# Message stages of a two-layer graph network: row loads and stores of sums issued one per step instead of in groups

## The reference

```python
edge_index = jnp.stack([src, dst])
h = jnp.maximum(_layernorm(x, axis=-1), 0.0)
x = x + _L0_gnn_ref(h, node_vec1, edge_attr_16, edge_attr_4, src, dst, ...)
h = jnp.maximum(_layernorm(x, axis=-1), 0.0)
x = x + _L1_gnn_ref(h, edge_attr_3, edge_attr_64, ..., edge_index)
# the core of layer 1 (layer 0 is alike, with the mean instead of a sum over 32)
w = jax.nn.relu(edge_feature @ W_fc1) @ W_fc2
xs, xv = s[dst], v[dst]
tp = jnp.concatenate([w0 * xs, w3 * einsum(xv, sh1), w1 * xs * sh1, w2 * xv, w4 * cross(xv, sh1)], axis=-1)
agg = jax.ops.segment_sum(tp, src, num_segments=N) / DENOM
```

## Time and profile before

| | |
|---|---|
| time, median of 3 runs | 10098.53 us (10094.6 to 10099.18) |
| the profiled execution, span | 12165.8 us |
| layer 0 messages, stretch read | 3000 to 7500 us |
| layer 1 messages, stretch read | 8600 to 11800 us |
| mean granted TensorE clock | 0.763 |

### The profile page before, as it was taken

The page is one execution under the profiler, slowest core; times in us unless marked ns, Lnnn a source line. Parts: engine busy times, 40 slices in busy tenths (PEclk is TensorE's granted clock), DMA queues, the critical chain, the costliest instruction groups (busy, mean ns, idle before and its releaser), DMA issues. The chain is left out here.

```text
span 12165.8 us, 170335 instructions
## 1 busy us (share of the span) xinstructions
PE 7197.2 (59%) x31160; PEld 4885.2 (40%) x31160; DVE 7321.5 (60%) x20980; ACT 4968.3 (41%) x16490; POOL 7606.9 (63%) x7069
## 2 busy tenths in 40 slices
PE   4444444444555555555555555676777777777778
PEld 3222222222222222222222222454666666766667
DVE  6444444445665666656656665665667666766664
ACT  2333333333333333333333333343555555545543
POOL 3666666656666666766666666555666666666660
PEclk7555555557777777777777777787888888888889
DMA  2222222223333333433333335444444434434365
GB/s 79 72 72 74 72 71 73 73 69 107 114 114 113 116 112 115 117 113 114 116 113 115 113 116 109 121 144 126 121 118 120 119 116 121 119 115 119 115 112 166
DMA packets 850560, 1315.71 MB, mean 108 GB/s; under 512 B 252608, under 2 KB 651712, under 8 KB 850368
## 3 DMA queue, kind: packets, MB, share of 16 engines
q0 software_dynamic: 337920, 667.48, 19.8%
q1 hardware_dynamic: 438416, 547.38, 15.3%
q10 hardware_dynamic: 74160, 100.15, 2.5%
HBM read 862.45 MB, written 914.08 MB: 146 GB/s over the span
## 5 line engine op out<-in xcount | busy, mean ns | idle before, releaser
L1425 POOL DMA_INDIRECT feat_m<-feat_tab,rows_m x3712 | 4206.2, 1133 | 2025.3 <-issue 1291.5
L1524 PE MATMUL pair<-prod_m,hot_m 128*128 128x160 f32 x14848 | 2529.9, 332 | 924.5 <-DVE prod_m L1743 644.4
L1524 PEld LDWEIGHTS pair<-prod_m,hot_m 128*128 128x128 f32 x14848 | 2359.4, 214 | 1095.3 <-issue 1095.0
L1557 ACT ACTIVATE prod_m<-part_m,rows_m 128x64 f32<-128x64 f32 x5568 | 1430.4, 337 | 2687.9 <-DVE part_m L1729 1348.3
L1545 ACT ACTIVATE hot_m<-hot_m,rows_m 128x128 f32<-128x128 f32 x5568 | 1727.7, 388 | 1721.2 <-DVE hot_m L1712 1279.8
L638 POOL DMA_INDIRECT sorted_rows<-rows_e,place_e x1664 | 1656.5, 996 | 1056.3 <-issue 526.8
L1775 DVE SCALAR_TENSOR_TENSOR acc_m<-acc_m,same_block,pair 128x640 f32<-128x640 f32 (+1 forms) x1392 | 1129.3, 811 | 1509.8 <-remote 735.7
L1501 PE MATMUL pair<-prod_m,hot_m 128*128 128x449 f32 x1856 | 1035.3, 691 | 1255.9 <-issue 716.3
L1444 POOL DMA_INDIRECT sorted_rows<-later_m,place_m x1248 | 1326.5, 1063 | 720.2 <-issue 354.3
L1501 PE MATMUL bank<-prod_m,hot_m 128*128 128x449 f32 x1856 | 1022.0, 683 | 951.2 <-DVE acc_m L1775 329.3
L1743 DVE TENSOR_TENSOR prod_m<-rows_m,feat_m 128x192 f32<-128x192 f32 (+2 forms) x4640 | 1214.9, 311 | 0.0
(11 more groups left out here) (244 smaller groups left out, 9374.9 us busy)
## 6 DMA issues: line engine op xcount, KB each, us to landing
agg_tab<-acc_m ACTq DMA_DIRECT2D x928, 320.0 KB
rows_m<-sorted_rows SPq DMA_DIRECT2D x928, 229.0 KB
agg_tab<-acc_m ACTq DMA_DIRECT2D x928, 224.5 KB
rows_m<-sorted_rows SPq DMA_DIRECT2D x928, 197.0 KB
feat_m<-feat_tab,rows_m POOLq DMA_INDIRECT x3712
turned_m<-in_turned ACTq DMA_DIRECT2D x159, 256.0 KB
agg_s<-agg_tab SPq DMA_DIRECT2D x98, 320.0 KB, 2.8
sorted_rows<-rows_e,place_e POOLq DMA_INDIRECT x1664
```

Of the source, the lines that this page charges most:

```text
L1425: pool.indirect_dma_start(out=feat[s % RING][:, k, :], out_offset=None, in_=g.feat_tab[l.n], in_offset=bass.IndirectOffsetOnAxis(ap=rows[s ...
L1524: mm = pe.matmul(dst, hot[s % l.hot_bufs][:, k, q, :], rhs, start=(k == 0 and col == 0), stop=(k == ST_TILES - 1), skip_group_check=True)
L1557: ins = act.activation(prod[s % prods][:, k, at:at + S0], part[s % 2][:, k, 0:S0], ACT.Copy, scale=rows[s % HELD][:, k, l.sh_at + m:l.sh_a ...
```

## The change

SP's body is called for every step and loads one step's rows, behind a wait of its own for the sum of the step 12 before (the one whose buffer it overwrites); the addresses are still read for four steps at once, in every fourth step, behind the wait as before, and are held in registers over the four steps. ACT's store is issued for one step at a time behind its own wait; the table's fields are still read for two or four steps at once, and now ahead of the wait. The age of a store in layer 1 becomes 8 steps for all (10, 9, 8 and 7 before), in layer 0 6 for all (6 and 5 before).

```diff
-L1.accs, L1.stores, L1.store_lag = 12, 4, STORE_LAG
+L1.accs, L1.stores, L1.store_lag = 12, 4, 8
...
-            def group(step, it, s):
-                if s % GROUP or (step is not None and step >= NST):
+            first = [None] * GROUP
+
+            def load(step, it, s):
+                if step is not None and step >= NST:
                     return
-                u = it * TURN + s
+                u, n, slot = it * TURN + s, s % GROUP, s % HELD
                 if step is None or step >= HELD:
-                    sp.wait_ge(acc_ready, u + GROUP - HELD + 1)
+                    sp.wait_ge(acc_ready, u - HELD + 2)
                     settle(sp, g.passed)
-                _, first = nc.values_load_multi_w_load_instructions(
...
-                for n in range(GROUP):
-                    slot = (s + n) % HELD
-                    sp.dma_start(rows[slot][:, :, :],
...
+                if n == 0:
+                    _, first[:] = nc.values_load_multi_w_load_instructions(
...
+                sp.dma_start(rows[slot][:, :, :],
...
             def store(step, it, s):
-                if s % l.stores or (step is not None and not l.store_lag - l.stores < step < NST + l.store_lag):
+                if step is not None and not l.store_lag <= step < NST + l.store_lag:
                     return
-                u = it * TURN + s
-                done = u + l.stores - l.store_lag
-                act.wait_ge(acc_ready, done + 1 if step is None or done < NST else NST + 1)
+                u, n = it * TURN + s, s % l.stores
+                if n == 0:
+                    _, fields[:] = nc.values_load_multi_w_load_instructions(
...
+                act.wait_ge(acc_ready, u - l.store_lag + 2)
                 settle(act, g.passed)
-                _, fields = nc.values_load_multi_w_load_instructions(
...
-                for n in range(l.stores):
...
-                    q = (s + n - l.store_lag) % l.accs
...
+                q = (s - l.store_lag) % l.accs
...
```

More of the change, by code:

```diff
@@ L1398, in _ @@
         def _(sp):
-            def group(step, it, s):
-                if s % GROUP or (step is not None and step >= NST):
+            first = [None] * GROUP
+            def load(step, it, s):
+                if step is not None and step >= NST:
                     return
-                u = it * TURN + s
+                u, n, slot = it * TURN + s, s % GROUP, s % HELD
                 if step is None or step >= HELD:
-                    sp.wait_ge(acc_ready, u + GROUP - HELD + 1)
+                    sp.wait_ge(acc_ready, u - HELD + 2)
                     settle(sp, g.passed)
-                _, first = nc.values_load_multi_w_load_instructions(
-                    g.first_row[0:1, bass.ds(u, GROUP)], engines=[mybir.EngineType.SP], min_val=0, max_val=E_PAD - ST,
-                    skip_runtime_bounds_check_because="the table's rows are cut off there")
-                for n in range(GROUP):
-                    slot = (s + n) % HELD
-                    sp.dma_start(rows[slot][:, :, :],
-                                 g.sorted_rows[l.n][bass.ds(first[n], ST), :].rearrange("(p k) w -> p k w", k=ST_TILES)
-                                 ).then_inc(rows_here[slot], 16)
-            turns(sp, STEPS, TURN, group, upto=NST // TURN)
+                if n == 0:
+                    _, first[:] = nc.values_load_multi_w_load_instructions(
+                        g.first_row[0:1, bass.ds(u, GROUP)], engines=[mybir.EngineType.SP], min_val=0, max_val=E_PAD - ST,
+                        skip_runtime_bounds_check_because="the table's rows are cut off there")
+                sp.dma_start(rows[slot][:, :, :],
+                             g.sorted_rows[l.n][bass.ds(first[n], ST), :].rearrange("(p k) w -> p k w", k=ST_TILES)
+                             ).then_inc(rows_here[slot], 16)
+            turns(sp, STEPS, TURN, load, upto=NST // TURN)
         @block.gpsimd
@@ L1537, in _ @@
         def _(act):
+            fields = [None] * (2 * l.stores)
             def scale_hot(step, it, s):
@@ L1607, in store @@
             def store(step, it, s):
-                if s % l.stores or (step is not None and not l.store_lag - l.stores < step < NST + l.store_lag):
+                if step is not None and not l.store_lag <= step < NST + l.store_lag:
                     return
-                u = it * TURN + s
-                done = u + l.stores - l.store_lag
-                act.wait_ge(acc_ready, done + 1 if step is None or done < NST else NST + 1)
-                settle(act, g.passed)
-                _, fields = nc.values_load_multi_w_load_instructions(
-                    g.table[0:1, bass.ds(u + STORE_LAG - l.store_lag, l.stores), :].rearrange("p u c -> p (u c)"),
-                    engines=[mybir.EngineType.Activation], min_val=0, max_val=SPARE,
-                    skip_runtime_bounds_check_because="the table holds block numbers and flags")
@@ L1618, in store @@
-                for n in range(l.stores):
-                    if step is not None and not 0 <= step + n - l.store_lag < NST:
-                        continue
-                    q = (s + n - l.store_lag) % l.accs
[L1622 to L1625, removed]
+                u, n = it * TURN + s, s % l.stores
@@ new lines, in store @@
+                if n == 0:
+                    _, fields[:] = nc.values_load_multi_w_load_instructions(
+                        g.table[0:1, bass.ds(u + STORE_LAG - l.store_lag, l.stores), :].rearrange("p u c -> p (u c)"),
+                        engines=[mybir.EngineType.Activation], min_val=0, max_val=SPARE,
+                        skip_runtime_bounds_check_because="the table holds block numbers and flags")
+                act.wait_ge(acc_ready, u - l.store_lag + 2)
+                settle(act, g.passed)
@@ L1627, in step_ @@
+                q = (s - l.store_lag) % l.accs
+                last = nc.s_assert_within(fields[2 * n + 1], 0, 1,
+                                          skip_runtime_bounds_check_because="the table holds flags here")
+                act.dma_start(g.agg_tab[l.n][bass.ds(fields[2 * n] * P, P), :], acc[q][:, :],
+                              cond=last).then_inc(acc_stored[q], 16)
             def step_(step, it, s):
```

## The result

| | before | after |
|---|---|---|
| median | 10098.85 us (10094.6 to 10113.94, 4 runs) | 10036.34 us (10016.41 to 10050.39, 4 runs) |
| ratio | | 0.9938 [0.9922, 0.9954] |
| profiled execution, span | 12165.8 us | 10014.7 us |

What follows compares the result with a forecast made beforehand. The prediction took POOL to bound layer 0, and DVE and PE holding each other to bound layer 1. Loads -2 and odd stores -8 gave -10 us on the median 10098.53, so 10,090 us; range 9,925 to 10,150.

Steps and rivals of the forecast that it cites:

- burst rival: Layer 1: four loads at once stall DVE's add-up 3.12 us in one group of four; 181 us faster, 9,918; chance 0.28.
- Layer 0 goes at POOL's pace: Layer 0: POOL's work and issuing fill 3972 of 4500 us, 88%, with occasional waits for DVE and ACT.
- the 8 us for the odd stores: ACT in layer 0: odd steps' stores now stand behind `place`, shortening POOL's wait; 8 us gained, at most 22.
- In layer 1 DVE and PE hold each other, POOL has slack: Layer 1: DVE waits 555.8 us for PE, PE 602.4 for DVE; POOL waits 488.9, so it has slack.
- The profiled execution is not the timed one: Whole kernel: 2067 us between profiled span and median, mostly laid to the profiled execution; the sum assumed to carry over.
- no measurable change: Whole kernel: the forecast of -10 us, under the 0.2% or some 20 us that can be told; chance 0.40.
- The loads are on nobody's path: SP's row loads: POOL waits only 24.0 us and DVE 3.3 us in all for loaded rows.
- More waits on SP and ACT, 0: SP and ACT queues, both layers: added waits cost 0; without cover 107 us on SP, 89 us on ACT.
- Loads earlier, -2 us: SP's loads leave singly, three of four one to three steps earlier; 2 us gained, of at most 27.
- Lockstep: Layer 0 groups: queues slowed to 0.70 us an instruction make added instructions cost 193 us, 10,290; chance 0.08.
- late stores: Layer 0: odd steps' stores land too late for DVE's add-up; 127 us slower, 10,226; chance 0.07.
- TensorE's clock: PE in layer 1: granted clock shifts, 27 us per hundredth; 10,065 or 10,120; chance 0.09 up, 0.08 down.

Runs made afterwards that it cites:

- before again: The kernel before, with no edit, profiled a second time: 10089.68 us against 10077.63, ratio 1.0009, profiled span 10087.4 us.
- the combination: The whole change with layer 0's loads put back into groups of four, against the kernel before: 12154.04 us, ratio 0.9996, on a slower chip.

## Why the prediction was right and wrong

The median was predicted 54 us too high and its direction as none. The range held the result because it reached down for the burst rival, and that rival's mechanism was another than the real one: this much was luck. By the prediction's steps:

- **Layer 0 goes at POOL's pace.** Right, and more so than read: before again has no wait for `place` worth the name (4.9 us in 16 times, where the earlier trace rows had 323.9). So the 8 us for the odd stores were not there to gain.
- **In layer 1 DVE and PE hold each other, POOL has slack.** This step failed. POOL sets the pace there too. The reading was right for its trace, but a step takes 3.69 us in it and 2651.6 / 928 = 2.86 in before again, whose span, 10087.4 us, is near the timed runs. DVE isn't busier in the first trace (7321.5 us in all against 7313.5), it stands idle longer, 413.2 us of it for "remote", a wait that before again doesn't have; so POOL had 488.9 us of slack there, and at 2.86 us a step it has 47.5. Every price that was set to nothing for "POOL and ACT have slack" hung on it.
- **The profiled execution is not the timed one.** It wasn't, but not because it was profiled. Timed runs on two other chips take 12167.53 and 12089.47 us. It goes with the chip; what makes these chips slower no run shows. The 2067 us between span and median were seen and put down to the profile; that a sum made on such a trace carries over as a difference was the assumption that broke. On the slower chips themselves "no measurable change" came true for the combination (0.9996); the whole change wasn't run there. Even the sort, which the change doesn't touch, took 2838 us in the first trace and 2330 in before again.
- **The loads are on nobody's path.** Right by waits (POOL waited 62.3 us for rows before, 70.6 after), wrong as a conclusion. A transfer that nobody waits for can still decide when two other engines meet. That was the missing term, in the traces -90 us in layer 1 and +20 to +27 in layer 0; the sum had -2 for the loads.
- **More waits on SP and ACT, 0.** SP: nothing seen. ACT: nothing in the whole change, +27 us with grouped loads (12 of which can come without an edit), within the bound of 89.
- **Loads earlier, -2 us.** Right for the earliness: without any lead the gain is the same. "Singly", which the same term held, was worth the 85 us.
- **The burst rival.** Right in direction, at a chance of 0.28. Its mechanism, DVE stopped for 3.12 us while SP issues, and its 181 us came from one group of the slower trace; before again has neither such stretches nor waits on "remote" in layer 1. What grouped loads do is to make the gathers of one step in four take 2.51 us instead of 2.0 to 2.2: about 85 us in the timed runs, half of its price.
- **Lockstep, late stores, TensorE's clock.** None seen: moves stay at 29 to 38 ns, no wait of DVE for a store shows in layer 0, the clock is 0.828 and 0.824.

Shown: the gain is SP's, in layer 1, from single issue and not from lead, sits in the length of POOL's gathers, and goes away when DVE's products go away; and a long gather is one that waits for the end of DVE's run of products. Argued, not shown: how four loads at once bring gathers and products together more often. Likely, the late features of steps 2 and 3 shift DVE's products so that the next gathers begin beside them. The two kernels that would have told it ran where the pattern is absent. Why single loads cost layer 0 some 23 us wasn't tried.

## What to carry to other kernels

Before reading who bounds a stage, hold the profiled span against the timed median: where it lies 20% above, as here, profile the kernel again, since the slack in that trace is not the slack of the timed runs. An engine whose busy time changes with its count unchanged may be held up by a partner that no wait names; look at its single instructions, by step and by what they end with. Loads in groups can cost nothing in waits for the loads and still 3% of a stage by the rhythm they set; the right grain differed between two stages of the same loop, so try it for each stage.

## What the runs showed of the hardware that was not expected

The same kernel takes 10,071 and 10,078 us on two chips and 12,089 and 12,168 on two others, and each chip's runs of it lie within 0.9% of each other. (The first runs, 10,099 us, have no chip on record.) On the slower ones every part but the last is longer (sort 2330 to 2838 us, layer 0 4079 to 4812, layer 1 2652 to 3409), and queue instructions come in stretches of 0.70 us: 345 of the 1856 moves of L1411 take over 0.6 us in the trace of before, none in before again. Layer 1's granted clock was 0.88 against 0.98.

A gather's instruction on POOL takes 0.946 us at the median and at most 1.22 when DVE has one product to a step; with six it takes 0.970 at the median and up to 2.5. One that is caught by the six products ends 0.82 us after the last of them, in every one of the 323 over 1.3 us to within 0.02 us.

DMA share and speed go apart: with the same bytes and 90 us less time, single loads raise the DMA share of layer 1 from 0.53 to 0.60. The loads' queue takes 31.8% of the DMA engines' time in layer 1 of after and 23.7% in before again for the same bytes to within 0.4%, and the stage is still shorter.
